# State update of a chunked linear attention: 4 products of 128 key columns by 64 value columns in place of 16 of 32 by 16

## The chip, the cores and the metric

The kernel runs on one core of one Trainium2 chip, in float32 throughout the part that this case is about. The metric is the time of one execution on the device in microseconds (us); the median of three executions of the kernel before is 1401.23 us.

## The reference, cut to what matters

Four layers in a row, each added to its input after a normalization: windowed attention, a mixture of experts, a linear attention with a causal mask, and a gated recurrence. The change is in the third. It has 2 sequences of 2048 tokens, 16 heads of 16 dimensions; queries and keys are doubled to 32 by a rotation:

```
q = silu(x @ Wq); k = silu(x @ Wk); v = x @ Wv      # split in 16 heads of 16
q, k = lrpe(q), lrpe(k)                             # [t cos, t sin]: 32 columns a head
energy = einsum('bhnd,bhmd->bhnm', q, k) * tril     # no softmax
out = einsum('bhnm,bhmd->bhnd', energy, v)
...
out = out @ Wo * sigmoid(x @ G1 @ G2), layernorm, residual
```

Since there is no softmax, the part of `out` that comes from earlier tokens is q times a running state, the sum over earlier tokens of k (outer product) v: for each head a block of 32 by 16.

## The kernel before

The work on this layer and on the recurrence is one stage, built by `attention_recurrence` (semaphores and tensors with the prefix `la`). It goes over NT = 32 tiles of 128 tokens, alternately of the one and of the other sequence (`B[i % 2]` holds the buffers of each). The program is a software pipeline written out by hand: at step s each engine's function (`tensor`, `vector`, `scalar`, `gpsimd`, `sync`) does one part of tile s-4, another of tile s-5, and so on; the order of the code is the order of the engine's queue, and semaphores tie the engines together.

What TensorE does for the attention in one step, in order:

- for tile s-4 the projections (L1655 queries and keys, L1660 values and gate) into the banks `bE[:, 0]` and `bE[:, 1]`;
- for tile s-5 the four products of the old state with the turned queries (L1683) and sixteen of masked energy with values (L1688), both into `bO`; after them semaphore `O`;
- for tile s-5 the **state update** (L1694), sixteen products, one for each head h = 4c + r: its 32 key columns of `kr` as the stationary operand, its 16 value columns as the moving one, into partitions 32r to 32r+31 and columns 16c to 16c+15 of `bE[:, 2]`; after them semaphore `U`;
- for tile s-4 one transpose (L1701), then products of the recurrence (L1517, L1514, L1528, L1532: one weight block of 128x128 and 128 moving columns each), the output projection (L1722), the gate (L1726), transposes (L1621, L1577), four transposes each of the rotated queries and keys (L1739, L1747), the sixteen energy products (L1768), and again the recurrence.

Each float32 product of TensorE stands in the trace as two records (a weight load under PEld and a matmul under PE each); a transpose is one record.

Semaphore `U` is waited for by VectorE, which in four instructions (L1877), one for each quarter of the partitions, adds the diagonal blocks to `state`, an array [128, 4, 64] in which head 4c + r has partitions 32r to 32r+31 and columns 16r to 16r+15 of chunk c, with zeros elsewhere; by GpSimd ahead of the gather of a later tile's expert rows (L2130); and, two tiles on, by VectorE before it overwrites `kr` (in `rotated`) and ScalarE before it overwrites `v`. VectorE's semaphore `st` is then waited for by the transposes L1739 of the next tile, which reuse `bE[:, 2]`.

`v` is [128, 16 heads, 32]: an even head has its 16 values in the first half of its 32 columns, an odd one in the second, and the other half is zero, so that the value columns of a pair of heads lie at 0 to 15 and 48 to 63 of 64.

Of the kernel before, what the change touches and what calls it, by code (L numbers as in the profile page):

```python
# [7 lines left out]
P = 128  # L8
# [3 lines left out]
ALU = mybir.AluOpType  # L12
# [4 lines left out]
HEADS, WIN = 16, 64  # L17
# [21 lines left out]
def chunks(ap, k):  # L39
    return ap.rearrange("p (k n) -> p k n", k=k)  # L40
# [18 lines left out]
def tile(step, lag, n):  # L59

    return (step - lag,) if 0 <= step - lag < n else ()
# [1296 lines left out]
def attention_recurrence(nc, A, W, Sw, xn1T, x1, ysh, yg, weight, place, tables, K, T, C, KC, ROOM, SLOTS, MIXED, later, wide, X):  # L1358
# [4 lines left out]
    CH = 4  # L1363
    HD = C // HEADS
# [12 lines left out]
    with memory(nc, "la") as (sb, ps):  # L1377
# [41 lines left out]
        bG, bH, bE = ps("G", [P, 512]), ps("H", [P, 512]), ps("E", [P, 4, 512])  # L1419
# [9 lines left out]
        def late(s):  # L1429

            return tuple(range(2 * s, 2 * s + 2)) if 0 <= s < 3 else (s + 3,) if 3 <= s < LATE - 3 else ()

        def late_banks(j):

            return (bE[:, 0], bE[:, 3], bE[:, 2, 0:C]) if j < 6 and j % 2 else (bG[:], bH[:], bO[:, C:2 * C])
# [199 lines left out]
        def tensor(e, ahead):  # L1635
# [7 lines left out]
            for s in range(STEPS):  # L1643
# [3 lines left out]
                for i in tile(s, 4, NT):  # L1647
                    d = B[i % 2]
# [5 lines left out]
                    for k in range(KC):  # L1654
                        o = e.matmul(bE[:, 0], d["xnT"][:, k, :], wqk[:, k, :], start=(k == 0), stop=(k == KC - 1))  # L1655
# [3 lines left out]
                    for k in range(KC):  # L1659
                        o = e.matmul(bE[:, 1, 0:C + HD], d["xnT"][:, k, :], wvg[:, k, 0:C + HD], start=(k == 0),  # L1660
                                     stop=(k == KC - 1))
# [6 lines left out]
                for i in tile(s, 5, NT):  # L1668
                    d = B[i % 2]
                    for r in range(4):  # L1670
                        e.wait_ge(S[f"em{r}"], i + 1)
                    for j in late(s - 1):
                        e.wait_ge(S["fo"], j + 1)
                    if i == 0:
                        e.wait_ge(S["zero"], 6)
                    if i >= 1:
                        e.wait_ge(S["oT"], i)
                    if i >= 2:
                        e.wait_ge(S["st"], i - 1)
                    for t in tile(s, 10, NT):  # L1680
                        e.wait_ge(S["nc"], t + 1)
                    for c in range(CH):
                        e.matmul(bO[64 * (c % 2):64 * (c % 2) + 64, (c // 2) * P:(c // 2 + 1) * P],  # L1683
                                 d["state"][:, c, :], d["qT"][:, c, :], start=(c < 2), stop=False,
                                 skip_group_check=True)
                    for h in range(HEADS):
                        g = h // 2 % 4
                        o = e.matmul(bO[32 * g:32 * g + 32, (h // 8) * P:(h // 8 + 1) * P], d["v"][:, h, :],  # L1688
                                     d["em"][:, h % 4, h // 4, :], start=False, stop=(h >= HEADS - 8),
                                     skip_group_check=True)  # L1690
                    o.then_inc(S["O"], 1)
                    for h in range(HEADS):
                        r, c = h % 4, h // 4
                        o = e.matmul(bE[32 * r:32 * r + 32, 2, c * HD:(c + 1) * HD], d["kr"][:, 32 * h:32 * h + 32],  # L1694
                                     d["v"][:, h, HD * (h % 2):HD * (h % 2) + HD], start=True, stop=True,
                                     skip_group_check=True)
                    o.then_inc(S["U"], 1)
                for i in tile(s, 4, NT):
                    e.wait_ge(S["hg"], i + 1)
# [18 lines left out]
                for i in tile(s, 5, NT):  # L1718
                    d = B[i % 2]
                    e.wait_ge(S["oT"], i + 1)  # L1720
                    for k in range(KC):
                        o = e.matmul(bE[:, 3, 0:C], d["oT"][:, k, :], wo[:, k, :], start=(k == 0), stop=(k == KC - 1))  # L1722
# [7 lines left out]
                for i in tile(s, 4, NT):  # L1730
                    d = B[i % 2]
# [6 lines left out]
                    for c in range(CH):  # L1738
                        o = e.transpose(bE[:, 2, c * P:(c + 1) * P], d["qr"][:, c * P:(c + 1) * P], ident)  # L1739
# [6 lines left out]
                    for c in range(CH):  # L1746
                        o = e.transpose(bE[:, 3, c * P:(c + 1) * P], d["kr"][:, c * P:(c + 1) * P], ident)  # L1747
# [13 lines left out]
                for i in tile(s, 4, NT):  # L1761
                    d = B[i % 2]
# [3 lines left out]
                    for c in range(CH):  # L1766
                        for r in range(4):
                            o = e.matmul(bE[:, r, c * P:(c + 1) * P], d["kT"][32 * r:32 * r + 32, c, :],  # L1768
                                         d["qT"][32 * r:32 * r + 32, c, :], start=True, stop=True)
# [4 lines left out]
                for j in late(s):  # L1774
# [3 lines left out]
                    for f in range(SK):  # L1778
                        o = e.matmul(late_banks(j)[2], FG[j % 2][:, f, :], sw2[:, f, :], start=(f == 0), stop=(f == SK - 1))
                    o.then_inc(S["fy"], 1)  # L1780
                if s == 8:
                    gates.wait(e)
                    for g, n in enumerate(G):
                        for m in range(KC):
                            for k in range(KC):
                                o = e.matmul(bH[:, g * KC + m:g * KC + m + 1], w["u" + n][:, k, m * P:(m + 1) * P],
                                             c0[:, k:k + 1], start=(k == 0), stop=(k == KC - 1))
# [20 lines left out]
        def vector(e):  # L1808
# [3 lines left out]
            for s in range(STEPS):  # L1812
                if s == 2:
                    experts_end(e)
                for i in tile(s, 5, NT):
                    d = B[i % 2]
# [14 lines left out]
                for t in tile(s, 10, NT):  # L1831
                    d, p, u = B[t % 2], H[t // 2 % 2], t // 2
# [4 lines left out]
                    if t % 2 == 0:  # L1837
# [3 lines left out]
                        for m in range(KC):  # L1841
                            o = e.scalar_tensor_tensor(p["c1"][:, m], f[:, m], c0[:, m:m + 1], d["ig"][:, m],
                                                       ALU.mult, ALU.add)
# [12 lines left out]
                for u in pair(s, 13):  # L1856
                    p = H[u % 2]
                    if u >= ON_ACT:
                        e.wait_ge(S["rsh"], 2 * ON_ACT + 2 * u + 2)
                    for q in range(2):  # L1860
                        if ON_ACT <= u < PAIRS - 1:
                            o = e.tensor_scalar(p["h"][:, q], p["h"][:, q], p["hmv"][:, q, 0:1], p["hrs"][:, q:q + 1],
                                                ALU.subtract, ALU.mult)
# [6 lines left out]
                for i in tile(s, 5, NT):  # L1870
                    st = B[i % 2]["state"]
                    if i == 0:
                        e.wait_ge(S["zero"], 6)
                    e.wait_ge(S["U"], i + 1)
                    for r in range(4):
                        at_r = slice(32 * r, 32 * r + 32)
                        o = e.tensor_tensor(st[at_r, :, HD * r:HD * r + HD], st[at_r, :, HD * r:HD * r + HD],  # L1877
                                            chunks(bE[at_r, 2, 0:CH * HD], CH), ALU.add)
                    o.then_inc(S["st"], 1)
                for i in tile(s, 1, NT):  # L1880
                    d, L, t = B[i % 2], i % 2, i // 2 + i % 2 * PAIRS
# [14 lines left out]
                for i in tile(s, 5, NT):  # L1896
                    d = B[i % 2]
# [11 lines left out]
                for u in pair(s, 12):  # L1909
                    p = H[u % 2]  # L1910
                    e.wait_ge(S["h"], u + 1)
                    for q in range(2):
                        o = e.bn_stats(p["hst"][:, q], p["h"][:, q])
                    o.then_inc(S["mvh"], 1)
                    e.wait_ge(S["mvh"], 2 * u + 1)
                    for q in range(2):
                        o = e.bn_aggr(p["hmv"][:, q], p["hst"][:, q])
                    o.then_inc(S["mvh"], 1)
                    if u == PAIRS - 1:

                        e.wait_ge(S["mvh"], 2 * u + 2)
                        for q in range(2):
                            o = e.tensor_scalar(p["h"][:, q], p["h"][:, q], p["hmv"][:, q, 0:1], None, ALU.subtract)
                        o.then_inc(S["hc"], 1)
                for i in tile(s, 6, NT):
                    d, n = B[i % 2], B[i % 2]["ln1"]
# [16 lines left out]
                for u in pair(s, 11):  # L1943
                    p = H[u % 2]
# [268 lines left out]

        S |= {"later": later.sem, "wide": wide.sem, "gates": gates.sem}
        return tensor, vector, scalar, gpsimd, sync, S


# [49 lines left out]
```

## Time and profile before

| | |
|---|---|
| median of three executions | 1401.23 us (1401.22 to 1401.35) |
| the profiled execution | 1399.33 us, of which 1397.5 us is the span that the trace covers |
| mean granted clock of TensorE | 0.997 of full speed |
| TensorE (PE) busy | 1358.4 us, 97% of the span |
| weight loads (PEld) | 1166.4 us, 83%, beside the matmuls |
| VectorE, ScalarE, GpSimd busy | 66%, 51%, 44% |
| state update (L1694) | 1024 matmul records in 32 tiles, first at 914.0, last at 1350.3 us |

The last stage takes the span from about 890 us to the end. Durations of single matmul records overlap, since they are pipelined; what a group takes of TensorE's time is read from its start to the start of the next group.

### The profile page before, as it was taken

The page shows a single profiled execution, that of the slowest core. Times are in us where ns is not written, and L with a number is a line of the kernel's source. Part 1 is how long each engine was busy: PE and PEld are TensorE (multiplying, and loading weights), DVE is VectorE, ACT ScalarE, POOL GpSimd, SP SyncE. Part 2 cuts the span into 40 slices and gives each one's busy share as a digit, 9 for nine tenths or more (in the row PEclk, how much of TensorE's full clock was granted, in tenths as well). Part 3 has the DMA queues.
Part 4 walks back from the last instruction along what each step waited for, and adds up shares of the span by engine and source line. Part 5 has one row for each costly group of instructions (what it writes and reads, how often), then busy time and mean ns, then how long its engine had stood idle before and what let it go on. Part 6 is the DMA issues. An engine that isn't in the chain of part 4 may idle for free.

```text
span 1397.5 us, 37478 instructions
## 1 busy us (share of the span) xinstructions
PE 1358.4 (97%) x13436; PEld 1166.4 (83%) x13436; DVE 928.2 (66%) x2185; ACT 712.3 (51%) x1706; POOL 609.0 (44%) x1146
## 2 busy tenths in 40 slices
PE   7999999999999999999999999999999999999995
PEld 6888888788988888888888899877788888888885
DVE  5888888475355555555555532367888888888764
ACT  4666666313444444444444333345566666666653
POOL 3656656233212112212111110645677877777443
PEclk9999999999999999999999999999999999999998
DMA  5433434362111111111111112541121122111000
GB/s 165 128 112 110 135 114 127 93 205 81 39 39 47 42 42 51 42 43 37 52 36 46 47 58 71 161 133 58 50 59 47 58 59 69 48 54 51 9 10 31
DMA packets 88726, 99.93 MB, mean 72 GB/s; under 512 B 12577, under 2 KB 75809, under 8 KB 88545
## 3 DMA queue, kind: packets, MB, share of 16 engines
q1 hardware_dynamic: 80928, 78.92, 18.1%
q0 software_dynamic: 6240, 17.05, 4.3%
q8 instruction: 111, 1.82, 0.6%
q10 hardware_dynamic: 1376, 1.57, 0.3%
q14 instruction: 71, 0.57, 0.1%
HBM read 63.68 MB, written 33.82 MB: 70 GB/s over the span
## 4 chain that ended last, share of the span: by engine, by line
PE 92%; ACT 2%; issue 2%; DVE 2%; POOL 1%; DVEq 0%; ACTq 0%; DMA 0%; POOLq 0%; SPq 0%
PE wa_Y L1202 11%; PE wa_P L1060 11%; PE wa_qv L1060 6%; PE la_E L1655 4%; PE wa_xk L1060 4%; PE la_G L1528 3%; PE la_E L1768 2%; PE wa_Y L450 2%; PE wa_S L1089 2%; PE wa_xk L501 2%; PE la_O L1688 2%; PE wa_S L437 2%; PE wa_qv L510 2%; PE la_E L1660 2%; PE la_O L1528 2%; PE wa_Z L475 2%
## 5 line engine op out<-in xcount | busy, mean ns | idle before, releaser
L1024 POOL COPY slot_idx<-source 128x1 int32<-128x1 int32 x58 | 21.3, 366 | 391.2 <-PE wa_Z L1193 376.2
L1060 PE MATMUL wa_P<-ex_xT,lane_w 128*128 128x128 f32 x1440 | 170.7, 275 | 0.0
L1202 PE MATMUL wa_Y<-w,ex_gT 128*128 x720 | 166.2, 380 | 1.4 <-DVE ex_gT L1274 1.0
L1060 PEld LDWEIGHTS wa_P<-ex_xT,lane_w 128*128 128x128 f32 x1440 | 165.7, 192 | 0.2 <-issue 0.2
L1202 PEld LDWEIGHTS wa_Y<-w,ex_gT 128*128 128x128 f32 x720 | 132.1, 190 | 18.8 <-issue 3.0
L1060 PEld LDWEIGHTS wa_qv<-ex_xT,lane_w 128*128 128x128 f32 x720 | 90.7, 191 | 17.9 <-issue 17.4
L1060 PE MATMUL wa_qv<-ex_xT,lane_w 128*128 128x128 f32 x720 | 103.6, 280 | 0.0
L1272 DVE TENSOR_TENSOR ex_gT<-ex_gT,wa_xk 128x256 f32<-128x256 f32 x60 | 25.1, 418 | 103.6 <-ACT ex_gT L1234 103.6
L1232 ACT ACTIVATE ex_gT<-wa_qv 128x256 f32<-128x256 f32 x60 | 23.1, 384 | 138.1 <-PE wa_qv L1060 138.0
L1056 ACT COPY lane_w<-w 128x1408 f32 x60 | 82.0, 1366 | 6.3 <-issue 1.0
L2130 POOL DMA_INDIRECT la_a<-yg,place x64 | 65.6, 1026 | 43.0 <-DMA yg<-ex_yo 17.6
L1821 DVE TENSOR_TENSOR la_em<-la_E,consts 128x512 f32<-128x512 f32 x128 | 79.1, 680 | 5.3 <-PE la_E L1768 5.0
L1346 POOL TENSOR_TENSOR la_ln_rs<-la_ln_ve,consts 128x1 f32<-128x1 f32 x128 | 76.9, 601 | 10.6
L1026 POOL DMA_INDIRECT slot_xa<-xn,slot_idx x58 | 69.6, 1200 | 15.9 <-POOL slot_idx L1024 15.9
L1232 ACT ACTIVATE ex_gT<-wa_P 128x384 f32<-128x384 f32 x60 | 29.5, 491 | 90.3 <-PE wa_P L1060 88.0
L1342 POOL TENSOR_SCALAR la_ln_ve<-la_ln_mv 128x1 f32<-128x1 f32 x128 | 30.4, 237 | 98.3 <-DVE la_ln_mv L1335 91.9
L1078 DVE COPY stage<-w 128x352 f32 (+1 forms) x96 | 34.7, 361 | 56.9 <-PE wa_S L1089 33.9
L1056 DVE COPY lane_w<-w 128x1408 f32 x60 | 53.9, 898 | 14.8 <-issue 7.7
L1060 PE MATMUL wa_xk<-ex_xT,lane_w 128*128 128x128 f32 x480 | 63.4, 275 | 0.0
L1655 PE MATMUL la_E<-la_wqk,la_xnT 128*128 128x512 f32 x128 | 61.3, 601 | 1.1 <-DVE la_em L1821 1.1
L1060 PEld LDWEIGHTS wa_xk<-ex_xT,lane_w 128*128 128x128 f32 x480 | 58.4, 192 | 0.0
L2025 ACT ACTIVATE la_c<-la_O,la_bs 128x128 f32<-128x128 f32 x64 | 20.0, 365 | 60.0 <-PE la_O L1528 43.4
(329 smaller groups left out, 3526.1 us busy)
## 6 DMA issues: line engine op xcount, KB each, us to landing
yg<-ex_yo SPq DMA_DIRECT2D x60, 128.0 KB, 1.7
w<-in_w SPq DMA_DIRECT2D x16, 384.0 KB, 4.8
w<-in_w SPq DMA_DIRECT2D x16, 352.0 KB, 3.0
w<-in_w SPq DMA_DIRECT2D x16, 320.0 KB, 4.1
wa_xa<-in_x SPq DMA_DIRECT2D x32, 128.0 KB, 2.1
x<-wa_xo SPq DMA_DIRECT2D x32, 128.0 KB, 1.7
xn<-wa_xn SPq DMA_DIRECT2D x32, 128.0 KB, 2.0
xn1T<-wa_x1T SPq DMA_DIRECT2D x32, 128.0 KB, 2.4
```

What stands on the lines that cost most here:

```text
L1026: e.indirect_dma_start(d["xa"][:], None, xn1, bass.IndirectOffsetOnAxis(ap=d["idx"][:, 0:1], axis=0)).then_inc(S[f"xa{i % 2}"], 16)
L1056: (e.tensor_copy(dst, src) if k else e.copy(dst, src)).then_inc(S[done], 1)
L1060: o = e.matmul(out, lane_w[:, i % 2, k, at:at + P], B[i % 2]["xT"][:, k, :], start=(k == 0), stop=(k == KC - 1))
L1078: e.tensor_copy(stage[:, j:j + 1, 0:b - a], w13[:, bass.ds(x, 1), k, a:b])
L1202: o = e.matmul(yb[:, 0:C], gT[:, k, :], w2[:, bass.ds(KF * y + k, 1), :], start=(k == 0), stop=(k == KF - 1))
L1232: o = e.activation(d["gT"][:, c0:c1], chunks(hb[2 * half][:, 0:n], c1 - c0), ACT.Silu)
L1342: e.tensor_scalar(ln.ve[:], ln.mv[:, 1:2], LN_EPS, None, ALU.add).then_inc(S[f"rs{tag}"], 1)
L1346: e.tensor_tensor(ln.rs[:], ln.ve[:], half, ALU.pow).then_inc(S[f"rs{tag}"], 1)
L1528: z = e.matmul(o, w["w" + name][:, k, m * P:(m + 1) * P], WT[t % 4][:, k, :], start=(k == 0), stop=(t % 2 == 0 and k == KC - 1))
L1655: o = e.matmul(bE[:, 0], d["xnT"][:, k, :], wqk[:, k, :], start=(k == 0), stop=(k == KC - 1))
L1821: e.tensor_tensor(d["em"][:, r], chunks(bE[:, r], CH), bc(K["causal"], 1, CH), ALU.mult).then_inc(S[f"em{r}"], 1)
L2130: e.indirect_dma_start(YG[k][i % 4][:], None, yg, bass.IndirectOffsetOnAxis(ap=place[:, k, t:t + 1], axis=0)).then_inc(S[f"a{k}{i % 4}"], 16)
```

## The change

The sixteen products become four, one for each chunk c of four heads: all 128 key columns of the chunk are the stationary operand, and the 64 value columns of the same four heads the moving one, picked out of `v` by a view that skips the zero halves. Each product gives all 16 combinations of four heads' keys with four heads' values; only the four on the diagonal are used. The result takes columns 64c to 64c+63 of `bE[:, 2]` in place of 16c to 16c+15, in all 128 partitions, and VectorE's four additions pick the 16 columns of their own head from each 64.

```diff
-                    for h in range(HEADS):
-                        r, c = h % 4, h // 4
-                        o = e.matmul(bE[32 * r:32 * r + 32, 2, c * HD:(c + 1) * HD], d["kr"][:, 32 * h:32 * h + 32],
-                                     d["v"][:, h, HD * (h % 2):HD * (h % 2) + HD], start=True, stop=True,
-                                     skip_group_check=True)
+                    own = d["v"][:].rearrange("p (b h) (x d) -> p b (h x) d", h=2, x=2)[:, :, 0:4:3, :]
+                    for c in range(CH):
+                        o = e.matmul(bE[:, 2, c * 64:(c + 1) * 64], d["kr"][:, c * P:(c + 1) * P],
+                                     own[:, 2 * c:2 * c + 2], start=True, stop=True)
                     o.then_inc(S["U"], 1)
...
                         o = e.tensor_tensor(st[at_r, :, HD * r:HD * r + HD], st[at_r, :, HD * r:HD * r + HD],
-                                            chunks(bE[at_r, 2, 0:CH * HD], CH), ALU.add)
+                                            chunks(bE[at_r, 2, 0:CH * 64], CH)[:, :, HD * r:HD * r + HD], ALU.add)
```

TensorE's queue around the update in one step of the steady part, before (sizes are output partitions x moving columns; the number at the end counts products):

```order
L1660 MATMUL la_E<-la_wvg,la_xnT 128x272 x2
L1683 MATMUL la_O<-la_qT,la_state 64x128 x4
L1688 MATMUL la_O<-la_em,la_v 32x128 x16
L1694 MATMUL la_E<-la_v,la_kr 32x16 x16
L1701 MATMUL la_E<-consts,la_hg 128x128
L1517 MATMUL la_G<-la_wT,gw_wf 128x128 x4
```

And the same place of the changed kernel:

```order
L1660 MATMUL la_E<-la_wvg,la_xnT 128x272 x2
L1683 MATMUL la_O<-la_qT,la_state 64x128 x4
L1688 MATMUL la_O<-la_em,la_v 32x128 x16
L1694 MATMUL la_E<-la_v,la_kr 128x64 x4
L1700 MATMUL la_E<-consts,la_hg 128x128
L1517 MATMUL la_G<-la_wT,gw_wf 128x128 x4
```

Nothing else changes its place on any engine: the full-width operations now begin one group earlier, at L1694 instead of L1701. Lines after L1694 have a number lower by one.

## Rows read from the trace of the kernel before

**Rows 1.** The page: busy time, share of the span, instructions.

```profile
PE 1358.4 (97%) x13436; PEld 1166.4 (83%) x13436; DVE 928.2 (66%) x2185; ACT 712.3 (51%) x1706; POOL 609.0 (44%) x1146
```

**Rows 2.** Busy time of each engine in a stretch of the last stage.

```profile
1150.00:1200.00 50.00, 50.00 (x633) 41.89 (x632) 42.16 (x109) 32.79 (x91) 38.08 (x73) 1.00 0.18 52
```

**Rows 3.** Waits of TensorE, 880 us to the end: total, times, longest.

```profile
PE la_E L1768 <- ACT la_kT L2009: 4.4, 6, 0.9
...
PE la_E L1655 <- DVE la_em L1821: 1.1, 1, 1.1
```

**Rows 4.** Timeline of TensorE, one step: start, duration, group, records.

```profile
1166.46 1.12 PE L1688 MATMUL la_O<-la_em,la_v 128*32 128x128 f32 x32
1167.36 0.51 PE L1694 MATMUL la_E<-la_v,la_kr 128*32 128x16 f32 x32
1167.80 0.33 PE L1701 MATMUL la_E<-consts,la_hg 128*128 128x128 f32 x1
1167.97 1.06 PE L1528 MATMUL la_G<-la_wT,gw_wf 128*128 128x128 f32 x8
1168.86 1.06 PE L1528 MATMUL la_G<-la_wT,gw_wi 128*128 128x128 f32 x8
```

**Rows 5.** Timeline of TensorE: weight blocks of 128x128, one moving column.

```profile
963.76 0.95 PE L1786 MATMUL la_H<-gw_c_start,gw_uf 128*128 128x1 f32 x8
964.57 1.03 PE L1786 MATMUL la_H<-gw_c_start,gw_ui 128*128 128x1 f32 x8
965.47 1.03 PE L1786 MATMUL la_H<-gw_c_start,gw_uc 128*128 128x1 f32 x8
966.36 1.96 PE L1655 MATMUL la_E<-la_wqk,la_xnT 128*128 128x512 f32 x4
```

**Rows 6.** Groups of weight loads, last stage: busy us, mean ns of one.

```profile
L1528 PEld LDWEIGHTS la_O<-la_wT,gw_wc 128*128 128x128 f32 x240 | 30.2, 191 | 3.1
...
L1694 PEld LDWEIGHTS la_E<-la_v,la_kr 128*32 128x32 f32 x1024 | 16.7, 110 | 0.0
```

**Rows 7.** Timeline of TensorE: two groups with wide moving operands.

```profile
1163.14 1.88 PE L1655 MATMUL la_E<-la_wqk,la_xnT 128*128 128x512 f32 x4
1164.86 1.08 PE L1660 MATMUL la_E<-la_wvg,la_xnT 128*128 128x272 f32 x4
```

**Rows 8.** Timeline of TensorE in the last tile with an update.

```profile
1349.94 0.51 PE L1694 MATMUL la_E<-la_v,la_kr 128*32 128x16 f32 x32
1350.38 1.16 PE L1514 MATMUL la_G<-la_c,gw_uf 128*128 128x128 f32 x8
1351.38 1.06 PE L1514 MATMUL la_G<-la_c,gw_ui 128*128 128x128 f32 x8
```

**Rows 9.** Timeline of TensorE: transposes.

```profile
1157.40 0.60 PE L1739 MATMUL la_E<-consts,la_qr 128*128 128x128 f32 x4
1157.83 0.60 PE L1747 MATMUL la_E<-consts,la_kr 128*128 128x128 f32 x4
```

**Rows 10.** Timeline of TensorE, first stage: L437 reads its moving operand with gaps.

```profile
159.16 1.09 PE L437 MATMUL wa_S<-wa_km,wa_qT 64*64 64x256 f32 x16
160.20 1.13 PE L450 MATMUL wa_Y<-wa_vb,wa_pT 128*64 128x34 f32 x32
```

**Rows 11.** Timeline of all engines in an early step, around the wait for kT.

```profile
931.59 0.59 PE L1726 MATMUL la_E<-la_g,la_hT 128*128 128x256 f32 x2
...
932.22 0.38 ACT L2099 ACTIVATE la_gt<-la_E 128x256 f32<-128x256 f32 x1 [2.15 <-PE la_E L1726]
...
934.16 1.17 PE L1768 MATMUL la_E<-la_qT,la_kT 32*128 32x128 f32 x32 [0.88 <-ACT la_kT L2009]
```

**Rows 12.** VectorE and GpSimd behind the update: timeline, and GpSimd's waits.

```profile
1167.95 0.91 DVE L1877 TENSOR_TENSOR la_state<-la_state,la_E 32x64 f32<-32x64 f32 x4 [0.96 <-PE la_E L1694]
```

```profile
POOL la_a L2130 <- PE la_E L1694: 11.0, 5, 4.0
```

## The prediction

> **What bounds the kernel now.** I read the page first: TensorE is busy for 97% of the span, the next engine 66% [rows 1]. The same in stretches of the last stage: in the steady part TensorE is busy 50.00 of 50 us at full clock, VectorE 42 [rows 2]. Then TensorE's waits, because the matmuls' ends are modelled and a full row could hide a stall: over the whole last stage it waits 4.4 us in six steps for the turned keys and once 1.1 us for the masked energy, and little else [rows 3]. So TensorE sets the pace where the change is made, and the question is how long the update holds it. That is read from start to start. The old update starts at 1167.36, the transpose behind it at 1167.80, the next group at 1167.97 [rows 4]: 0.44 us for 32 records (13.8 ns each), 0.17 for the transpose, 0.61 together. The steps are alike; there are 32 updates.
>
> **What the change removes.** 32 records of 32 weight columns and 16 moving columns, 0.44 us. They are this cheap for one reason: each uses one quarter of the array's columns, and four go side by side. A weight load of 32 columns lasts 110 ns and one of 128 columns 191 [rows 6], so 96 more columns take 81 ns, 0.84 ns each, and 32 columns stream in 27 ns. One behind the other, 32 such loads would take 0.86 us; the row shows half of that.
>
> The Trainium skill ("TensorE: Matmul & The Clock Gate", LDWEIGHTS) gives a load its columns divided by 1.2 GHz, whatever the rows. By that rule alone 32 loads of 32 columns and 8 of 128 both take 0.853 us, and the change would be worth nothing; the slope of [rows 6] agrees with the rule, the 0.44 us of [rows 4] doesn't, and the measurement decides for the old form.
>
> **What it adds.** 8 records of 128 weight columns and 64 moving columns in full-width mode. Two limits:
>
> - The moving side: 4 records of 512 columns take 1.72 us [rows 7], 430 ns a record, 0.84 ns a column. 64 columns then take 54 ns, 8 records 0.43 us.
> - The weight side: the trace has this load with nearly no moving side. 24 records with 128x128 weights and a single moving column go from 963.76 to 966.36 [rows 5], 108 ns each, as much as records with 128 moving columns (0.89 us for 8, 111 each [rows 4]). The stream of 107 ns from [rows 6] says the same. So in full width the loads are not overlapped with each other, and they, not the moving columns, set the pace below 128 columns: 8 x 0.108 = 0.87 us.
>
> I take the weight side: [rows 5] is the nearest row, with the same weights and a moving side on the other side of 64 from 128, and both neighbours give nearly the same. Bounds for the group: 0.43 to 0.89 us.
>
> **What it moves.** The passage from column-tiled to full-width work costs something too. Behind the last update there is no transpose, and the first 8 full-width records take 1.00 us (1350.38 to 1351.38 [rows 8]) against 0.89 in mid-stream: 0.11. In front of a transpose it is smaller: 0.17 for L1701, against 0.43 / 4 = 0.11 for one of a row of transposes [rows 9], so 0.06. After the change the passage lies ahead of the update (0.11), and the transpose costs 0.11. Bounds of the passage: 0 (the first load slips in while L1688 ends) to 0.11.
>
> **The sum.** Per step: 0.11 + 0.87 + 0.11 = 1.09 us in place of 0.61, 0.48 more. For 31 steps 14.9 us. In the last tile no transpose follows: before, 1349.94 to 1351.38 is 1.44 us for update and the next 8 records; after, 0.11 + 0.87 + 0.89 = 1.87, 0.43 more. Together +15.3 us.
>
> **Whether all of it is on the path.** In the steady part yes, TensorE has no idle time [rows 2]. In the six early steps it could only be absorbed if what TensorE waits for were tied to something ahead of the update. It isn't: the wait for the keys ends after a run of ScalarE that begins when L1726 is done (ScalarE idles 2.15 us for it, starts at 932.22, and releases L1768 at 934.16 [rows 11]); L1726 stands behind the update in TensorE's queue, so the whole run slides. If a wait did absorb it, six times 0.48 is 2.9 us, my lower bound for this term. Ahead of the update nothing changes. After 1351 us the tail hangs on products behind the last update and slides with it.
>
> **What costs nothing.** VectorE waits 0.96 us for the update, then takes 0.91 us for its four additions [rows 12]. They read the same 64 elements from PSUM, now in four runs of 16, 64 apart; the trace has no pair that differs in this alone. If each were as much as 60 ns longer, that is 0.24 us in an engine that is busy 42 of 50 us, and it ends long before the next transposes into that bank (several us of recurrence, projection and gate products lie between). The update's end itself comes 0.5 us later after VectorE's previous work, but the products behind it come later too, so VectorE has the same distance to what it must be ready for. GpSimd waits for the update in five early steps, 11.0 us in all [rows 12]; its gathers, too, slide with TensorE. The view of `v` has runs of 16 values with gaps. The only priced gaps are those of L437 (runs of 64): 16 records of 256 columns in 1.04 us [rows 10], 65 ns a record with four parts of the array in parallel, against 430 / 2 / 4 = 54 from [rows 7]; at most a fifth more. At double the price for a column 64 columns would take 108 ns and still be under the load.
>
> Against the profile's own time: 1399.33 + 15.3 = 1414.6 us (span 1397.5 to 1412.8). The median stands 1.9 us above that execution, 1401.23; so 1416.5 us.
>
> **Rivals.** 0.2% (2.8 us) is about what a measurement of this kernel can tell from no change.
>
> *The moving side sets the pace (6%, no change).* If the next load hides under the current product, 8 records take 0.43 us; with passage and transpose 0.65 against 0.61, +1.3 us over 32 steps, 1402.5; without any passage cost 0.54, -2.2 us, 1399.0. For it: loads are drawn as overlapping the matmuls. Against it: the one-column rows [rows 5], where there is hardly a moving side and the pace is still 108 ns. The Trainium skill's load rule named above also ends here, at 0.
>
> *Each record costs the same (4%, faster).* If the old 13.8 ns were a fixed cost of a record, 24 fewer save 0.33 us a step; with 0.11 - 0.06 for the passage that is -0.28 x 32 = -9.0 us, 1392.2. It is decided by the pace of the new records: the change wins beyond 0.2% only if they come at under (0.61 - 0.09 - 0.22) / 8 = 37 ns. Against it: no full-width record in the rows comes at under 107 ns [rows 5, 9]. The Trainium skill ("TensorEngine Tiling (Array Packing)", Instruction Overhead) speaks for this side: about 60 cycles for each matmul, however few its columns, which at 2.4 GHz is 25 ns and would make the old group 0.80 us. The 13.8 ns of [rows 4] contradict it where four go side by side.
>
> *Gaps in the moving operand are dear (3%, much slower).* At four times a column's price a record takes 215 ns, the group 1.72 us, 0.85 more a step than forecast: 15.3 + 27.2 = +42.5 us, 1443.7. Only runs much shorter than L437's could do that.
>
> *Part is absorbed (5%, slower by less).* The waits of [rows 3] swallow their share and the passage costs 0.06: +15.3 - 2.9 - 1.6 = +10.8, 1412.0.
>
> *The forecast (82%).* 1416.5. Its own range: passage down to 0.06 (-1.6), records 108 to 111 ns (up to +0.8), L1701 keeping its 0.17 (+1.9), 1414.9 to 1419.2.
>
> **Numbers.** The range that leaves out no more than the moving-side, fixed-cost and gap cases (13%) runs from below the absorbed case to the top of the forecast's own: 1410 to 1420. Faster 0.04; same 0.06; slower 0.90.
>
> **What would show it.** In the changed trace the update has 8 records; from its start to that of L1700 some 0.9 us (0.43 if I am wrong on the side that limits); its loads last about 190 ns; from L1688's start to the update's 0.9 to 1.0; L1700 to the next group 0.11. A steady step grows by 0.48 us. VectorE's additions stay at about 217 ns, waits for the keys stay at 0.9. I am wrong if loads of successive full-width records overlap as soon as the moving side is longer than one column but shorter than 128, or if the array reads runs of 16 at a fraction of its pace.

## The result, and the profile after

In the first measurement the changed kernel takes 1421.97 us (median of four, 1419.52 to 1423.19) against 1401.29 (four, 1401.22 to 1401.67): ratio 1.0147, 95% interval 1.0135 to 1.0159, 20.7 us slower. A second and later one, with the changed kernel five times and the kernel before 17 times, gives 1420.56 (1418.99 to 1421.45) against 1403.02 (1400.41 to 1405.54): 1.0126, 1.0109 to 1.0142, 17.5 us. The kernel before spreads over 5 us there (five executions at 1400.4 to 1400.7, twelve at 1402.3 to 1405.5); the four executions of the first measurement lie between these two groups, close together. The forecast was 1416.5 us, +15.3. So its direction holds, its size is short by 2 to 5 us, and both medians lie above the 1420 us at which its range ended. Two things make that up: steps that grow by more than was reckoned, and TensorE's clock.

The page of the changed kernel (span 1421.4 us, time 1423.19), one stretch of the last stage (busy time of PE, PEld, DVE, ACT, POOL, then the granted clock), and TensorE's waits from 880 us on, in answer to [rows 1 to 3]:

```profile
PE 1382.5 (97%) x12668; PEld 1183.5 (83%) x12668; DVE 928.0 (65%) x2185; ACT 713.3 (50%) x1706; POOL 612.7 (43%) x1146
```

```profile
1150.00:1200.00 50.00, 50.00 (x507) 40.62 (x506) 40.14 (x103) 31.27 (x86) 40.02 (x74) 1.00 0.19 56
```

```profile
PE la_E L1767 <- ACT la_kT L2008: 4.4, 6, 0.9
...
PE la_E L1655 <- DVE la_em L1820: 1.1, 1, 1.1
```

TensorE has 768 records less and 24 us more of busy time. It is as full as before, and every wait that the profile marks is equally long: the longer update was not absorbed in any of them. (The forecast called the waits beside these two "little else"; they are 5.1 us in all, the same before and after.) The update's own instructions (count, shortest/median/longest in ns), and VectorE's additions behind it:

```profile
L1694 PEld LDWEIGHTS la_E<-la_v,la_kr x256: 186/192/192, 916.2 to 1374.1; 128*128 128x128 f32 x128
L1694 PE MATMUL la_E<-la_v,la_kr x256: 275/275/323, 916.2 to 1374.2; 128*128 128x64 f32 x128
```

```profile
L1876 DVE TENSOR_TENSOR la_state<-la_state,la_E x128: 207/217/228, 917.4 to 1375.2; 32x64 f32<-32x64 f32 x128
```

The additions take 217 ns as before, with the gaps in what they read. And one step of TensorE's timeline, to be laid beside [rows 4]:

```profile
1167.51 1.12 PE L1688 MATMUL la_O<-la_em,la_v 128*32 128x128 f32 x32
1168.56 1.10 PE L1694 MATMUL la_E<-la_v,la_kr 128*128 128x64 f32 x8
1169.50 0.28 PE L1700 MATMUL la_E<-consts,la_hg 128*128 128x128 f32 x1
1169.62 1.06 PE L1517 MATMUL la_G<-la_wT,gw_wf 128*128 128x128 f32 x8
```

Read from start to start: the products of energy and values (L1688) hold TensorE for 1.05 us in place of 0.90, the update for 0.94 in place of 0.44, the transpose for 0.12 in place of 0.17. From the start of L1688 to the group behind the transpose it is 2.11 us (2.10 in other steps) against 1.51: 0.59 more, where the forecast said 0.48. L1688 itself is not touched by the change, and it is the row that the forecast did not look at.

**Where the 23.9 us between the two spans went.** At the first energy products of the stage the changed kernel is 2.04 us late (909.32 against 907.28), before any update has run. At the end it is 23.86 us late (L1558, 1407.97 against 1384.11). Between them lies a step of 20.04 us, from update to update, that takes 16.12 in the kernel before; I come to it with the clock, and its excess over the growth of the other steps is 3.3 us. The rest, 18.5 us over 32 updates, is 0.58 us each. The same comes out where no clock falls on either side: `wide_after`, an experiment below, has none between these two places, nor has the kernel before (first pair of lines):

```profile
907.28 1.17 PE L1768 MATMUL la_E<-la_qT,la_kT 32*128 32x128 f32 x32 [0.88 <-ACT la_kT L2009]
1384.11 1.13 PE L1558 MATMUL la_E<-gw_uo,la_c 128*128 128x256 f32 x4 [1.11 <-DVE la_c L1852]
```

```profile
908.26 1.17 PE L1767 MATMUL la_E<-la_qT,la_kT 32*128 32x128 f32 x32 [0.88 <-ACT la_kT L2009]
1403.62 1.13 PE L1558 MATMUL la_E<-gw_uo,la_c 128*128 128x256 f32 x4 [1.11 <-DVE la_c L1852]
```

495.36 against 476.83 us, 18.5 more. So 18.5 us are the change's steps, and 5.3 us of the first pair of traces are something else: 3.3 in that step, 1.5 in a like place in the first half of the program, 0.5 scattered over code that is the same in both. Scatter of that kind is common: the eight traces without a fall at that place of the first half reach the first energy products between 906.97 and 908.66 us. Behind L1558 the clock falls in every trace, but that tail lasts 13.4 us in both kernels and costs nothing between them.

**A little is absorbed.** In the steady part one step in two grows from 14.09 to 14.68 us, by 0.59, and the other from 14.22 to 14.77, by 0.55. In the second kind a group of eight records (L1528) stands ahead of L1655. The kernel before, then `narrow`, an experiment below:

```profile
1147.84 1.16 PE L1528 MATMUL la_O<-la_wT,gw_wc 128*128 128x128 f32 x8
1148.98 1.96 PE L1655 MATMUL la_E<-la_wqk,la_xnT 128*128 128x512 f32 x4
```

```profile
1161.45 1.95 PE L1655 MATMUL la_E<-la_wqk,la_xnT 128*128 128x512 f32 x4 [0.16 <-DVE la_em L1820]
```

From L1528 to L1655 it is 1.13 to 1.16 us in the kernel before, 1.08 to 1.09 after, 1.00 with the update's products issued twice, and 1.31 in `narrow`, where the profile marks the wait: for VectorE's masking of the energies. In these steps L1655 starts 0.82 to 0.83 us behind the first of these operations, in the kernel before, the changed one and `narrow` alike. So TensorE waits a little for VectorE here even where no wait is marked, and the longer update eats some 0.04 us of that in each of nine steps, 0.4 us in all. The forecast had read the full row of [rows 2] as no idle time at all.

**The clock.** The stretch behind the start values of the recurrence (L1785, L1786 in the kernel before), in the changed kernel; beneath it the granted clock of TensorE in single microseconds, the third figure from the end:

```profile
969.90 1.34 PE L1785 MATMUL la_H<-gw_c_start,gw_uc 128*128 128x1 f32 x8
971.11 3.76 PE L1655 MATMUL la_E<-la_wqk,la_xnT 128*128 128x512 f32 x4
974.66 2.02 PE L1660 MATMUL la_E<-la_wvg,la_xnT 128*128 128x272 f32 x4
```

```profile
969.00:970.00 1.00, 1.00 (x11) 1.00 (x11) 0.99 (x2) 0.00 (x0) 0.80 (x3) 1.00 0.00 0
971.00:972.00 1.00, 1.00 (x3) 0.59 (x3) 0.61 (x3) 0.00 (x0) 0.99 (x2) 0.50 0.00 0
```

From about 970.5 to 977.5 us the granted clock is 0.50 (1.00 again from 978), 1.2 in place of 2.4 GHz, and L1655 takes 3.55 us to the next group. In the kernel before it takes 1.80, from 966.36 [rows 5] to

```profile
968.16 1.08 PE L1660 MATMUL la_E<-la_wvg,la_xnT 128*128 128x272 f32 x4
```

Ahead of the fall TensorE had idled 0.67 us, run 38 records of energies and recurrence in 2.5 us, and then most of 24 records with one moving column each (L1785, from 968.20 us). A second fall lies at 275 us, in the first half of the program, in which both kernels are the same; the trace of the kernel before has the same idle times there and no fall. The same products in the changed kernel, then in the kernel before:

```profile
274.65 4.20 PE L409 MATMUL wa_S<-stage,lane_w 128*128 128x256 f32 x12
278.68 1.89 PE L377 MATMUL wa_qv<-lane_w,stage 128*128 128x256 f32 x8
```

```profile
274.28 2.76 PE L409 MATMUL wa_S<-stage,lane_w 128*128 128x256 f32 x12
276.88 1.89 PE L377 MATMUL wa_qv<-lane_w,stage 128*128 128x256 f32 x8
```

L409 takes 4.03 us in the one and 2.60 in the other. The two falls are worth 3.3 and 1.5 us in this trace. In seven traces of the experiments the fall behind the one-column records is half as long and costs 1.7 us where it can be compared (the step is 18.41 us in `again`, against 16.72 in `wide_after`, which has none). Whether they come with the change or by chance was the first question for the experiments.

### The profile page after: what moved, and what is told of

The parts are those of the page before. It is cut to its first block, busy times and chain, and to the rows that moved or that the text cites. A ratio compares the mean times of both kernels' runs of the same rounds, so it can differ in the third digit from the quotient of the medians.

```text
span 1421.4 us, 35942 instructions
## 1 busy us (share of the span) xinstructions
PE 1382.5 (97%) x12668; PEld 1183.5 (83%) x12668; DVE 928.0 (65%) x2185; ACT 713.3 (50%) x1706; POOL 612.7 (43%) x1146
## 4 chain that ended last, share of the span: by engine, by line
PE 92%; issue 2%; ACT 2%; DVE 2%; POOL 1%; DVEq 0%; DMA 0%; POOLq 0%; SPq 0%; ACTq 0%
PE wa_Y L1202 11%; PE wa_P L1060 11%; PE wa_qv L1060 6%; PE la_E L1655 4%; PE wa_xk L1060 4%; PE la_G L1528 3%; PE la_E L1767 2%; PE wa_Y L450 2%; PE la_O L1688 2%; PE la_E L1694 2%; PE wa_S L1089 2%; PE wa_xk L501 2%; PE wa_S L437 2%; PE wa_qv L510 2%; PE la_E L1660 2%; PE la_O L1528 2%
## 5 line engine op out<-in xcount | busy, mean ns | idle before, releaser
L1202 PEld LDWEIGHTS wa_Y<-w,ex_gT 128*128 128x128 f32 x720 | 132.1, 190 | 18.9 <-issue 3.2
L1346 POOL TENSOR_TENSOR la_ln_rs<-la_ln_ve,consts 128x1 f32<-128x1 f32 x128 | 76.6, 599 | 10.7
L1342 POOL TENSOR_SCALAR la_ln_ve<-la_ln_mv 128x1 f32<-128x1 f32 x128 | 33.7, 263 | 104.4 <-DVE la_ln_mv L1335 98.0
L1655 PE MATMUL la_E<-la_wqk,la_xnT 128*128 128x512 f32 x128 | 63.1, 616 | 1.1 <-DVE la_em L1820 1.1
L1876 DVE TENSOR_TENSOR la_state<-la_state,la_E 32x64 f32<-32x64 f32 x128 | 27.8, 217 | 46.5 <-PE la_E L1694 45.2
```

Of the source, the lines that this page charges most:

```text
L1202: o = e.matmul(yb[:, 0:C], gT[:, k, :], w2[:, bass.ds(KF * y + k, 1), :], start=(k == 0), stop=(k == KF - 1))
L1342: e.tensor_scalar(ln.ve[:], ln.mv[:, 1:2], LN_EPS, None, ALU.add).then_inc(S[f"rs{tag}"], 1)
L1346: e.tensor_tensor(ln.rs[:], ln.ve[:], half, ALU.pow).then_inc(S[f"rs{tag}"], 1)
```

## The experiments

Stretches named below run on TensorE from the start of one group to the start of another, in the steady part of the last stage.

### Fewer moving columns

```diff
-o = e.matmul(bE[:, 2, c * 64:(c + 1) * 64], d["kr"][:, c * P:(c + 1) * P], own[:, 2 * c:2 * c + 2], start=True, stop=True)
+o = e.matmul(bE[:, 2, c * 64:c * 64 + HD], d["kr"][:, c * P:(c + 1) * P], d["v"][:, 4 * c, 0:HD], start=True, stop=True)
```

> Full-width form with the moving operand cut to the 16 columns of one head in each chunk (leaves out three of four heads of the update). Theory L (the weight load sets the pace): the update's 8 records take what they take with 64 columns, 0.94 us from the update's start to the transpose's, and the profile's step from the start of L1688 to the group behind the transpose stays at 2.10 us. Theory M (the 64 moving columns or their gaps cost something): the group gets shorter, to 0.7 us or less. If only the end of the group before is hidden differently, L1688 stays at 1.05 us.

```profile
1149.85 1.12 PE L1688 MATMUL la_O<-la_em,la_v 128*32 128x128 f32 x32
1150.89 1.06 PE L1694 MATMUL la_E<-la_v,la_kr 128*128 128x16 f32 x8
1151.81 0.31 PE L1700 MATMUL la_E<-consts,la_hg 128*128 128x128 f32 x1
1151.95 1.06 PE L1528 MATMUL la_G<-la_wT,gw_wf 128*128 128x128 f32 x8
```

A quarter of the moving columns, and the group takes 0.92 us in place of 0.94, the stretch 2.10 as before the cut. The weight load sets the pace, as forecast; the rival that the moving side does is out. 1421.56 us in one execution, 2.1 us above the next kernel although the stretch is the same: in every second step VectorE comes 0.22 us later to the masking of the energies, and L1655 waits for it (the line shown above). Why VectorE is later here is not shown.

### Adjacent moving columns

```diff
-own[:, 2 * c:2 * c + 2]
+d["v"][:, 4 * c:4 * c + 2]
```

> Full-width form with 64 adjacent columns of v as the moving operand in place of the four runs of 16 (the values are those of two heads and of the zeros between them, so the update is not that of the reference). Theory L: 0.94 us as now, step 2.10 us. Theory G (the gaps cost the missing 0.05 us): 0.89 us or less.

```profile
1164.85 1.10 PE L1694 MATMUL la_E<-la_v,la_kr 128*128 128x64 f32 x8
1165.79 0.28 PE L1700 MATMUL la_E<-consts,la_hg 128*128 128x128 f32 x1
```

0.94 us again. The runs of 16 with gaps between them cost nothing. 1419.50 us in one execution. Like `narrow`, this kernel doesn't compute the reference's update.

### The four products twice

```diff
-for c in range(CH):
+for c in (*range(CH), *range(CH)):
```

> Full-width form with the four products issued twice (same result). Theory P (the passage from column tiles to full width is a cost by itself, 0.20 us, and a record 0.111 us): the group grows from 0.94 to 1.83 us, +0.89, step 2.99 us. Theory R (full-width records with 64 columns are slower than those with 128): the group doubles, 1.88 us or more.

```profile
1163.05 1.12 PE L1688 MATMUL la_O<-la_em,la_v 128*32 128x128 f32 x32
1164.09 2.00 PE L1694 MATMUL la_E<-la_v,la_kr 128*128 128x64 f32 x16
1165.93 0.28 PE L1700 MATMUL la_E<-consts,la_hg 128*128 128x128 f32 x1
```

The second eight records cost 0.90 us (1.84 against 0.94), 112 ns each, and L1688 keeps its 1.04. Eight records at their pace are 0.89 us, so 0.05 us of the 0.94 and 0.15 us of L1688 are paid once, when the array goes over from column tiles to the full width: the passage is a cost by itself, of 0.20 us. 1447.46 us in one execution, 27.0 above the traced execution of `again` (1420.49), the changed kernel with a clock fall at the same place. That is less than 32 x 0.90 = 28.8: one step in two grows by 0.90 us and the other by 0.78, from 14.77 to 15.55, since the rest of the small wait ahead of L1655 is eaten up.

### Halfway: two heads in a product

```diff
-for c in range(CH):
-    o = e.matmul(bE[:, 2, c * 64:(c + 1) * 64], d["kr"][:, c * P:(c + 1) * P], own[:, 2 * c:2 * c + 2], start=True, stop=True)
+for c in range(CH):
+    for g in range(2):
+        o = e.matmul(bE[64 * g:64 * g + 64, 2, c * 32:(c + 1) * 32],
+                     d["kr"][:, c * P + 64 * g:c * P + 64 * g + 64], own[:, 2 * c + g], start=True, stop=True,
+                     skip_group_check=True)
```

VectorE's additions read the 32 columns of a product in place of 64 (left out here).

> Halfway form: 8 products of 64 key columns by 32 value columns, two side by side (same result). Theory L by the pace of L450 in the first stage (records of 64 weight columns, two side by side, 1.06 us for 32): 16 records take 0.53 us, plus part of a passage, step 1.7 to 1.85 us against 1.51 before and 2.10 after. If records were what costs (fixed price each), 16 records would take half of the old 0.44 us and the step would be under 1.4 us.

```profile
1160.74 1.12 PE L1688 MATMUL la_O<-la_em,la_v 128*32 128x128 f32 x32
1161.79 0.66 PE L1695 MATMUL la_E<-la_v,la_kr 128*64 128x32 f32 x16
1162.38 0.33 PE L1702 MATMUL la_E<-consts,la_hg 128*128 128x128 f32 x1
1162.54 1.06 PE L1517 MATMUL la_G<-la_wT,gw_wf 128*128 128x128 f32 x8
```

0.59 us for the group and 1.80 for the stretch, half of the way from 1.51 to 2.10; 1412.60 us in one execution, with one clock fall in it, at 275 us. Fewer and larger products are slower at each stage of the change, so records are not what costs. L1688 takes its 1.05 us here too: quarter tiles followed by half tiles are also a passage.

### The kernel before with one small product left

```diff
-for h in range(HEADS):
+for h in (HEADS - 1,):
```

> The kernel before with one of the 16 small products left in the update (leaves out the rest of it). Theory T (the small records hide the end of L1688's last records, so that the update cost less than its 0.44 us): from the start of L1688 to the group behind the transpose 1.2 us or more, in place of 1.51. The reckoning of the prediction (0.44 us for the update, 13.8 ns a record, nothing else): 1.51 - 0.42 = 1.09 us.

```profile
1152.25 1.12 PE L1688 MATMUL la_O<-la_em,la_v 128*32 128x128 f32 x32
1153.21 0.21 PE L1694 MATMUL la_E<-la_v,la_kr 128*32 128x16 f32 x2
1153.35 0.33 PE L1701 MATMUL la_E<-consts,la_hg 128*128 128x128 f32 x1
1153.51 1.06 PE L1517 MATMUL la_G<-la_wT,gw_wf 128*128 128x128 f32 x8
```

1.26 us, not the 1.09 that the prediction's reckoning gives. Taking 15 of the 16 products out saves 0.25 us a step, not 0.42, although the row of their group says 0.44. 1396.21 us in one execution, with a clock fall behind the one-column records; the kernel leaves 15 of 16 heads out of the update. The row of a group holds more than the group's own time, and the next experiment shows what.

### The two groups of column tiles in the other order

In the code before, the loop of L1694 is moved ahead of the loop of L1688; their line numbers change places.

> The kernel before with the two groups of column tiles in the other order: first the 16 small products of the update, then the 16 of 128 columns (same result). Theory T (the small records hide the end of the 128-column ones, which otherwise costs about 0.15 us): from the start of L1683 to the group behind the transpose 2.22 to 2.26 us in place of 2.10, about +4 to +5 us in all. Sum of the groups without hiding: 2.10 us, no change.

```profile
1152.77 0.66 PE L1683 MATMUL la_O<-la_qT,la_state 128*64 128x128 f32 x8
1153.35 0.45 PE L1688 MATMUL la_E<-la_v,la_kr 128*32 128x16 f32 x32
1153.63 1.14 PE L1694 MATMUL la_O<-la_em,la_v 128*32 128x128 f32 x32
1154.70 0.33 PE L1701 MATMUL la_E<-consts,la_hg 128*128 128x128 f32 x1
1154.86 1.06 PE L1517 MATMUL la_G<-la_wT,gw_wf 128*128 128x128 f32 x8
```

My expectation of 2.22 to 2.26 us failed: it is 2.09, as in the old order (2.10, 1165.87 to 1167.97 us). The 128-column tiles take 1.07 us here in place of 0.90, and the 32 small records 0.28 in place of 0.44. I had still taken the 0.44 for their own price. 1400.07 us in one execution, the fall at 966 us in it.

The starts of single records in the traces say where the time stands. Start of the last record of a group to the start of the first of the next, in ns, medians of the 23 to 25 steps between 990 and 1345 us, which agree within 3 ns:

| last record | first record of the next group | ns | trace |
|---|---|---|---|
| quarter tile, 128 moving columns (L1688) | the same tiling, 16 moving columns, in another column tile | 53 | before |
| the same | the same tiling, 16 moving columns, in the column tile of that last record | 109 | `one` |
| the same | full width, half tiles, or transpose | 203 | `after`, `narrow`, `twice`, `pairs`, `swap`, `front_update` |
| half tile, 128 moving columns (la_O<-la_qT,la_state) | quarter tiles | 202 to 203 | every trace |
| full width, 64 moving columns | half tiles | 205 | `front_update` |
| half tile, 32 moving columns | transpose | 153 | `pairs` |
| quarter tile, 16 moving columns | transpose | 113 | before, `one` |
| the same | the same tiling, 128 moving columns, in another column tile | 12 | `swap` |

Within a tiling the next group starts after 12 or 53 ns in another column tile and after 109 in the one that is still taken, and wherever the tiling changes after 113 to 205. From the first to the last start the 128-column records need 845 ns (865 in `swap`), and the small ones 332 behind the 128-column ones and 263 behind half tiles. So the old order's 0.90 is 845 + 53 and its 0.44 is 332 + 113, and the 0.28 of this kernel is 263 + 12. Of the 0.17 us between the two rows of the small group 0.10 is its passage to the transpose and 0.07 that its records start more slowly behind the 128-column ones. In this kernel those pay the passage, 203 ns, and from the same point the sum is the same: 53 + 332 + 113 against 263 + 12 + 20 + 203, both 498 ns.

### The full-width update in front

```diff
+for c in range(CH):
+    o = e.matmul(bE[:, 2, c * 64:(c + 1) * 64], d["kr"][:, c * P:(c + 1) * P], own[:, 2 * c:2 * c + 2], start=True, stop=True)
+o.then_inc(S["U"], 1)
 for c in range(CH):
     e.matmul(bO[64 * (c % 2):64 * (c % 2) + 64, (c // 2) * P:(c // 2 + 1) * P],
...
 e.wait_ge(S["U"], i + 1)
+e.wait_ge(S["O"], i + 1)
 for r in range(4):
```

The same four products no longer stand behind L1688; the second wait is VectorE's, ahead of its additions.

> The changed kernel with the four full-width products ahead of the state products instead of behind the energy products, so that they follow full-width work (same result; VectorE's addition waits for the state products as well). Theory T: the end of the 128-column tiles is exposed wherever a full-width group follows, be it the update or the transpose, so the stretch from the first of the three groups to the group behind the transpose stays at 2.65 to 2.7 us, as after the change (0.59 + 2.10). The reckoning of the prediction (0.11 ahead of full-width float32 products, 0.06 ahead of a transpose): update 0.89, then 0.59 + 0.89 + 0.17, 2.54 us.

```profile
1164.49 1.00 PE L1684 MATMUL la_E<-la_v,la_kr 128*128 128x64 f32 x8
1165.42 0.66 PE L1688 MATMUL la_O<-la_qT,la_state 128*64 128x128 f32 x8
1166.01 1.12 PE L1693 MATMUL la_O<-la_em,la_v 128*32 128x128 f32 x32
1167.06 0.33 PE L1700 MATMUL la_E<-consts,la_hg 128*128 128x128 f32 x1
1167.22 1.06 PE L1517 MATMUL la_G<-la_wT,gw_wf 128*128 128x128 f32 x8
```

2.73 us for the three groups and the transpose, against 2.70 in the changed order; the reckoning of the prediction says 2.54. The 128-column tiles take 1.05 us in front of the transpose as well. At this other place the update doesn't avoid the passage: the 128-column tiles pay it in front of the transpose. 1420.54 us in one execution, with both clock falls.

### The clock: both kernels again, and with a wider start group

> The changed kernel again, five rounds. Theory C (two falls of TensorE's clock make up what 32 longer steps don't): the times spread over 1419.5 to 1423.5 us, and the profile's clock falls to half in one or both of the stretches at 270 to 280 and 965 to 980 us. A time without either would be 1401.3 + 32 x 0.59 = 1420.2 or a little less. Rival: the whole 20.7 us comes from the steps, and the times stay at 1422.

> The kernel before again, for its clock. Theory C: the falls of the clock at 270 to 280 and 965 to 980 us are not the change's; most executions of the kernel before have one or both as well, so this trace shows at least one, and its time is 1402 to 1405 us. Rival: only the changed kernel has them, and this trace has the clock at 1.0 from 20 us to the last stage's end, 1401.3 us.

The kernel `again` is 1420.56 us (five executions, 1418.99 to 1421.45, lower than the 1419.5 to 1423.5 that I expected); its trace has no fall at 275 us and one behind L1785, where L1655 lasts 3.54 us. `before_again` is 1401.56 us in one execution, below the 1402 to 1405 that I expected. Its trace is unlike the first one of the same code:

```profile
274.91 4.27 PE L409 MATMUL wa_S<-stage,lane_w 128*128 128x256 f32 x12
```

The fall at 275 us is there without the change, and the one at 970 us is in the traces of `one` and `swap`, which differ from the kernel before only in the update group. Of the 17 executions of the kernel before in the second measurement the five at 1400.4 to 1400.7 us have a mean granted clock of 0.997 and the twelve at 1402.3 to 1405.5 us one of 0.994 or 0.995. The slower level goes with the lower clock; where in the program it fell in these executions is not on record. The rival, that only the changed kernel has the falls, is out.

Does the start group bring its fall about? In both kernels its one column was read 64 times (VectorE's addition behind it, left out here, reads the first of each 64):

```diff
-o = e.matmul(bH[:, g * KC + m:g * KC + m + 1], w["u" + n][:, k, m * P:(m + 1) * P], c0[:, k:k + 1], start=(k == 0), stop=(k == KC - 1))
+q = (g * KC + m) * 64
+o = e.matmul(bH[:, q:q + 64], w["u" + n][:, k, m * P:(m + 1) * P], c0[:, k:k + 1].broadcast_to([P, 64]),
+             start=(k == 0), stop=(k == KC - 1))
```

> The changed kernel, and the 12 products L1785 at the start of the recurrence read their one moving column 64 times (result as before, the additional columns are not used). Theory C1 (the group of one-column products is what lets the clock fall there): clock 1.0 all through 955 to 985 us, L1655 behind it at 1.8 us, and 1 to 3.5 us less than the changed kernel wherever that had fallen. Rival C2 (the stall and the transposes before it are to blame, or mere chance of timing): the fall stays as often.

```profile
968.86 1.06 PE L1786 MATMUL la_H<-gw_c_start,gw_uc 128*128 128x64 f32 x8
969.75 1.94 PE L1655 MATMUL la_E<-la_wqk,la_xnT 128*128 128x512 f32 x4
971.52 1.08 PE L1660 MATMUL la_E<-la_wvg,la_xnT 128*128 128x272 f32 x4
```

> The same edit on the kernel before. Theory C1: where the kernel before has no fall there (its profile has none), nothing changes, 1401.3 us; the difference between this and the changed kernel with the same edit is then 32 x 0.59 = 18.9 us. If the edit itself costs, it is 12 records wider groups at the same pace, under 0.2 us.

The wider group costs no more (2.6 us in all), and the clock stays up behind it in both traces, with the same 0.67 us of idle time ahead (the fall at 275 us is in that of `wide_before`). Of the eleven traces with one-column records eight have the fall behind them. The changed kernel takes 1418.84 us with it (five; four within 1418.5 to 1419.0, one at 1422.3), ratio to the kernel before 1.0119, 1.0102 to 1.0136, against 1.0126 without: the intervals overlap. The kernel before takes 1402.35 (twelve, 1399.88 to 1403.59), ratio 0.9992, 0.9982 to 1.0002. I had expected 1401.3 for it and a difference of 18.9; the medians differ by 16.5. Eight of its twelve executions lie 1.5 to 3.7 us above the lowest, so the wider group doesn't take the slower level away, and the one at 1422.3 us has the same mean clock, 0.996, as its four neighbours. The traces point to the one-column records as a cause of the fall behind them and don't prove it: if the five traces without that fall were spread by chance over all thirteen, both wide ones would be among them in 10 cases of 78, and the times can't tell 1 us. The two lowest times differ by 18.6 us in both pairs (1418.99 to 1400.41, and 1418.50 to 1399.88), beside the 18.5 us from the steps.

## Why the prediction was right and wrong

**Right: what bounds, and that nearly all of it is on the path.** TensorE is full before and after, its waits in the early steps stay at 4.4 us in six and 1.1 in one, these steps grow by 0.6 us like the others (13.44 to 14.04), and the tail slides. VectorE's additions stayed at 217 ns. Only the unmarked wait for the masked energy took 0.4 us.

**Right: the new records go at the pace of their weight load.** 0.87 us were forecast from 24 records with one moving column [rows 5], with 0.89 as the upper bound; 0.90 is what eight of them cost (`twice`), and 16 moving columns in place of 64 make no difference (`narrow`). The rivals of the moving side, of a price for each record and of gaps are all excluded, each by an experiment of its own (`narrow`, `pairs`, `contig`).

**Wrong: "After the change the passage lies ahead of the update (0.11)", the passage.** The sum had 0.11 for the passage (bounds 0 to 0.11), 0.87 for the records and 0.11 for the transpose, 1.09 us. The rows show 0.20 (0.15 under L1688, 0.05 under the update), 0.89 and 0.12, 1.21 us. So of the 0.12 us that a step's sum is short, 0.09 are the passage, the term that failed. In all the steps cost 18.5 us in place of 15.3.

The forecast read its 0.11 in the row of the group behind the small update [rows 8]. Most of a passage stands in the row of the group in front, as the time from its last record to the next start, and there it didn't look: 203 ns behind a record with 128 moving columns, 113 behind one with 16, 53 where the tiling stays. The change turns the 53 ns behind L1688 into 203. The 0.44 us for the old update was no price of its own for the same reason, since it holds the passage to the transpose. What the stretch would lose without the update is less: L1688 with a transpose right behind it would take 845 + 203 + 165 ns, 1.21 us (an estimate from the starts above and the 165 ns from transpose to next group in `swap`), so the old update costs 0.30 us and the new one 0.89.

Why a passage takes so long is shown in part. It is no fixed price: 90 ns lie between the last records with 128 and with 16 moving columns in the same tiling, and 112 columns at the 0.84 ns of [rows 7] are 94 ns (an estimate). The 109 ns after which `one` can use the column tile of L1688's last record are what 128 columns take at that price (107). So it fits the numbers that the last record runs out before the tiling changes and that some 0.1 us come on top, of which no run shows the cause; the half tiles of `pairs`, with 32 moving and 64 weight columns, need 153 ns, more than their moving columns explain. The Trainium skill ("TensorEngine Tiling (Array Packing)", Key Properties) says that changing the tiling mode drains TensorE. The traces agree, 203 ns against 53; the page has no price, and the prediction took one from behind a record with 16 moving columns.

**Missing: the clock.** The range ended at 1420 us and had no room for a clock that falls to 1.2 GHz for a few us in some executions. There was a sign of it: the profiled execution stood 1.9 us under the median, which the forecast added as a constant, and `before_again`, at 1401.56 us, has a fall worth 1.5 us. Of the 20.7 us of the first measurement 18.5 are the steps; the other 2.2 are of the size of the falls, but only one execution of each kernel is traced, the slowest of the changed kernel and one of the kernel before that was faster, at 1399.33 us, than its four; how the others divide is open. In the second measurement the interval of the ratio, 1.0109 to 1.0142, holds the steps alone (18.5 / 1401.3 = 1.3%). Without any fall the forecast would still be 3 us short, with a time of 1419.8 us, just inside the range of 1410 to 1420 us.

## What to carry to other kernels

A group of small products that sit side by side in the array's columns costs less than its full-width replacement as long as the weight load sets the pace: here 16 of 32x16 cost 0.30 us and 4 of 128x64 cost 0.89, with a quarter of the records. Before a group is replaced, read what its neighbours take in both tilings, since the start-to-start time of a group contains its passage to the next one; the price of a group is what the whole stretch loses when it is taken out. And a kernel whose times repeat to 0.03% in four executions may still have a second level, as this one has: look at the granted clock of its weak stretches before a range is drawn.

## What the hardware showed that I had not expected

- 32 records of 32 weight columns and 16 moving columns start every 8.5 ns behind half tiles (263 ns from first to last, `swap`) and every 10.7 ns behind quarter tiles with 128 moving columns (332 ns).
- Passing from column tiles with 128 moving columns to full width costs 0.20 us here, 0.15 before the first full-width record starts (203 ns in place of 53) and 0.05 in the group itself.
- Leaving a tiling takes longer the more moving columns its last record has: 203 ns with 128, 113 with 16, both in quarter tiles.
- The same program shows 1.0 or 0.5 of the clock in the same stretch in different executions: at 275 us (idle times of 0.96, 0.6 and 0.4 us among short groups) and at 970 us (0.67 us idle, 2.5 us of other records, then 24 one-column records); in the traces with a fall the clock was back at 1.0 in at most 7 us.
